# A selective scan taken by halves of the channels, with its decay in PSUM and another order on ScalarE

## The chip, the cores and the metric

The kernel runs on one core of one Trainium2 chip, as one program. The metric is the device time in microseconds (us). Its engines are TensorE (PE; PEld is its weight load), VectorE (DVE), ScalarE (ACT), GpSimd (POOL) and SyncE (SP).

## The reference

The program is eight stages: a Mamba-like selective scan, two kinds of mixture of experts, each twice, and three attention stages, over 1024 tokens of width 256. Each adds its result to the stream x. Only the first stage, the scan, is touched. With u the normed stream, delta a softplus of a small projection, and B and C two rows of 16 numbers for each token, it computes for each channel d and each of 16 states n

```python
def step(h, inp):
    u_t, delta_t, B_t, C_t = inp
    dA = jnp.exp(delta_t[:, :, None] * A)
    dBu = (delta_t * u_t)[:, :, None] * B_t[:, None, :]
    h = dA * h + dBu
    y_t = jnp.einsum('bdn,bn->bd', h, C_t)
    return (h, y_t)
```

and then y + u * D. The kernel here treats the 1024 tokens as two sequences of 512, in each of which the recurrence starts anew.

## The kernel before

The channels lie on the 128 partitions, as two halves (dc = 0, 1, NC = 2), and the tokens along the free axis, T = 1024 of them, as two sequences of SEQ = 512 (NSEQ = 2). The work of `selective_scan` has three parts.

**Ahead of the loop.** The stream is normed and transposed to g.xt, projected to `rows` (L313 copies them out of PSUM), and `rows` are projected to delta's argument in `wide` (L254). Softplus is made for each half of the channels in several steps: ScalarE takes Abs (L319), Exp (L324), Ln (L327) and Exp of the negative (L331), in each step for both halves before the next step; DVE takes the relu (L368), the correction for lost bits (L375 to L379), delta (L381) and delta times u, `du` (L382); POOL adds the two main parts (L230). Three table loads stand between ScalarE's steps (two of them ahead of L327 and L331, one ahead of the exponential of A, L321).

**The loop over the states.** It runs for n = 0 to 15, written as a hardware loop of 8 rounds with two states each (k = 0, 1). For a state:

- PE spreads row n of B and row n of C over all partitions, `spread` at L276, four bf16 matmuls of 512 columns into `wide[:, 0]` (B) and `wide[:, 1]` (C), B first. B waits until DVE has read the one before it (`driven`), C until ScalarE has copied the one before it (`copied`).
- ScalarE makes `decay` for both halves of the channels, exp(delta * A), 128x1024 each (L338), into SBUF, and then copies C's row out of PSUM into `cs` (L342), from which POOL reads it.
- DVE makes `drive` = du * B for both halves (L390, which reads B in PSUM), sets the decay at the first token of each sequence to zero (L393), and runs the recurrence over 1024 tokens for each half, `tensor_tensor_scan` at L398. All its operands but B lie in SBUF.
- POOL multiplies `state` with `cs` into `term`, for each half of the channels (L238), from SBUF to SBUF.
- PE adds `term` to `acc` in PSUM through the identity matrix in float32, `add_terms` at L284. An addition of one half of the channels is two matmuls in the program and four rows of the trace.

`decay`, `drive`, `state`, `term` and `cs` have two buffers each. PE's order is written out by hand: spread(n + 1), then add_terms(n). So PE spreads state n + 2 only once it has added state n.

**Behind the loop.** DVE adds u * D to `acc` (L406), PE transposes the result (L303), and DVE adds it to x (L411). The next stage begins with the norm at L106.

Of the kernel before, what the change touches and what calls it, by code (L numbers as in the profile page):

```python
# [5 lines left out]
F32 = mybir.dt.float32  # L6
BF16 = mybir.dt.bfloat16
# [5 lines left out]
P = 128  # L13
# [165 lines left out]
def selective_scan(nc, g, d):  # L179


    c = {n: Count(nc, n, p) for n, p in (
        ("loaded", 0), ("projected", 0), ("rows", 0), ("split", 0), ("dt", 0), ("soft_v", 0),
        ("size", 0), ("relu", 0), ("nega", 0), ("e", 0), ("lg", 0), ("over", 0), ("main", 0),
        ("ready", 0), ("spread_b", 0), ("spread_c", 0), ("copied", 0), ("decay", 0), ("driven", 0), ("state", 4),
        ("read", 4), ("summed", 4), ("gated", 0), ("turned", 0), ("zeroed", 0), ("selected", 0), ("added", 0))}
    HALF = 2 * N_STATE
    with (
        sbuf(nc, "xw", [P, NC, XROWS], F32) as xw,
        sbuf(nc, "dtw", [XROWS, H], F32) as dtw,  # L190
        sbuf(nc, "vecs", [P, 2 * NC + NC * N_STATE], F32) as vecs,
        sbuf(nc, "pick1", [3 * HALF, HALF], F32) as pick1,
        sbuf(nc, "pick", [3 * HALF, HALF, P], BF16) as pick,
        sbuf(nc, "rows", [XROWS, T], F32) as rows,
        sbuf(nc, "rest", [3 * HALF, T], F32) as rest,
        sbuf(nc, "part", [3 * HALF, T], BF16) as part,
        sbuf(nc, "stack", [3 * HALF, T], BF16) as stack,
        sbuf(nc, "nega", [P, NC, N_STATE], F32) as nega,
        sbuf(nc, "delta", [P, NC, T], F32) as delta,
        sbuf(nc, "du", [P, NC, T], F32) as du,  # L200
        sbuf(nc, "decay", [P, 2, NC, T], F32) as decay,
        sbuf(nc, "drive", [P, 2, NC, T], F32) as drive,
        sbuf(nc, "state", [P, 2, NC, T], F32) as state,
        sbuf(nc, "term", [P, 2, NC, T], F32) as term,
        sbuf(nc, "cs", [P, 2, T], F32) as cs,
        psum(nc, "acc", [P, NC, T], F32) as acc,
        psum(nc, "wide", [P, 2, T], F32) as wide,
        nc.Block() as block,
    ):
# [13 lines left out]
        def _(pool):  # L223
            pool.wait_ge(c["loaded"].sem, 64)
            pool.tensor_copy(pick[:, :, :], pick1[:, :].unsqueeze(2).broadcast_to([3 * HALF, HALF, P])) \
# [5 lines left out]
            pool.sem_inc(c["read"].sem, c["read"].prime)  # L231
            with pool.Fori(0, N_STATE // 2) as i:
                for k in range(2):
                    for dc in range(NC):
                        wait(pool, c["state"], 2 * k + dc + 1, i, 4)
                        wait(pool, c["copied"], k + 1, i, 2)
                        wait(pool, c["summed"], 2 * k + dc - 3, i, 4)
                        pool.tensor_tensor(term[:, k, dc, :], state[:, k, dc, :], cs[:, k, :], ALU.mult) \  # L238
                            .then_inc(c["read"].sem, 1)

        @block.tensor
        def _(pe):
# [3 lines left out]
            for s in range(NSEQ):  # L246
                for kc in range(NC):
                    last = pe.matmul(acc[0:XROWS, 0, s * SEQ:(s + 1) * SEQ], xw[:, kc, :],
                                     g.xt[:, kc, s * SEQ:(s + 1) * SEQ], start=(kc == 0), stop=(kc == NC - 1))
                last.then_inc(c["projected"].sem, 1)  # L250
# [1706 lines left out]
```

## Time and profile before

| | |
|---|---|
| median of 3 runs | 1935.83 us (1930.82 to 1942.93) |
| the profiled execution | 1939.39 us, span 1937.6 us |
| its mean granted clock of TensorE | 0.94 |
| PE, DVE, ACT, POOL busy over the span | 87%, 71%, 50%, 36% |
| the scan stage, up to the end of L411 | 198.5 us |

Times of rows are counted from the start of the span. A row gives a start, a duration, the engine, the line and the operation; x is how many instructions it groups; the brackets tell how long the engine had been idle and what released it. PEclk is the clock granted to TensorE, 1.00 for 2.4 GHz and 0.50 for 1.2 GHz.

### The profile page before, as it was taken

Reading aid. Unit: us, or ns where it says so; the run is one execution under the profiler, and the core shown is the slowest. Engines: PE = TensorE matmul, PEld = TensorE weight load, DVE = VectorE, ACT = ScalarE, POOL = GpSimd, SP = SyncE. Lnnn points to the kernel's source line nnn. Section 1 sums busy time; section 2 is a strip of 40 time slices with the busy share of each in tenths; the row PEclk is TensorE's granted clock in tenths of the full one; section 3 lists DMA queues with packets and bytes.
Section 4 is the critical chain, followed back from the end, with each engine's and each line's share of the span. In section 5 each row is a group of like instructions: output and inputs, shape, how many; then the busy total and the mean of one; then the engine's idle time right before and its main releaser. Section 6 shows DMA issues by size and latency. Waiting matters only on the chain. (4 is left out here: it accounts for less than half of the span.)

```text
span 1937.6 us, 35418 instructions
## 1 busy us (share of the span) xinstructions
PE 1688.6 (87%) x10848; PEld 1358.2 (70%) x10848; DVE 1380.8 (71%) x2841; ACT 976.3 (50%) x2160; POOL 691.8 (36%) x610
## 2 busy tenths in 40 slices
PE   2666799689999989989999998899799999888986
PEld 1222688567777978867777787777587888887764
DVE  6998666778887467677778747655788888657653
ACT  3432443377787344337778744111588888633111
POOL 1676122156665012216556512100355555303000
PEclk8788899899999989989999998999899999998998
DMA  0000111100000011110000004398211000011984
GB/s 29 0 0 0 47 49 49 47 20 16 22 16 1 1 55 43 46 50 25 22 14 24 4 1 119 106 258 257 74 28 30 30 27 16 1 66 54 260 243 145
DMA packets 39478, 111.15 MB, mean 57 GB/s; under 512 B 5504, under 2 KB 23664, under 8 KB 32240
## 3 DMA queue, kind: packets, MB, share of 16 engines
q1 hardware_dynamic: 39408, 110.26, 19.6%
q8 instruction: 39, 0.64, 0.1%
q14 instruction: 31, 0.25, 0.0%
HBM read 109.19 MB, written 1.05 MB: 57 GB/s over the span
## 5 line engine op out<-in xcount | busy, mean ns | idle before, releaser
L1294 POOL TENSOR_TENSOR xn<-xn 128x512 f32<-128x512 f32 x138 | 180.1, 1305 | 269.6 <-DVE xn L1189 269.6
L1280 POOL TENSOR_SCALAR prob<-prob,recip 128x256 f32<-128x256 f32 (+2 forms) x256 | 229.5, 913 | 69.7 <-DVE recip L1173 69.6
L1084 ACT ACTIVATE prob<-banks,peak 128x256 f32<-128x256 f32 (+3 forms) x384 | 190.5, 502 | 109.2 <-DVE peak L1164 103.6
L933 PE MATMUL banks<-pt,v 128*128 128x256 f32 (+3 forms) x768 | 204.3, 409 | 6.9 <-ACT pt L1019 6.9
L933 PEld LDWEIGHTS banks<-pt,v 128*128 128x128 f32 x768 | 145.2, 190 | 73.8 <-issue 31.8
L888 PE MATMUL banks<-k_hi,q_hi 128*128 128x256 f32 (+2 forms) x384 | 152.7, 398 | 27.9 <-DVE k_lo L1180 27.8
L1164 DVE TENSOR_REDUCE peak<-banks 128x1 f32<-128x256 f32 (+3 forms) x384 | 160.9, 446 | 18.1 <-PE banks L892 16.2
L568 POOL TENSOR_TENSOR gu_lo<-gu,gu_hi 128x512 fp32r<-128x512 f32 x36 | 46.7, 1298 | 295.2 <-ACT gu_hi L526 295.2
L909 PE MATMUL banks<-ident,prob 128*128 128x128 f32 x864 | 140.4, 279 | 3.2 <-DVE pt L1017 3.2
L1189 DVE TENSOR_TENSOR xn<-xn,ropes 128x512 f32<-128x512 f32 x138 | 124.3, 901 | 0.0
L1187 DVE TENSOR_TENSOR xn<-banks,ropes 128x512 f32<-128x512 f32 x138 | 95.2, 690 | 39.9 <-ACT xn L1052 39.6
L284 PE MATMUL acc<-term,ident 128*128 128x512 f32 x128 | 79.7, 771 | 50.2 <-POOL term L238 50.2
L537 ACT ACTIVATE silu<-gate 128x512 f32<-128x512 f32 x72 | 43.1, 599 | 159.3 <-PE up L489 159.1
L889 PE MATMUL banks<-k_lo,q_hi 128*128 128x256 f32 (+2 forms) x384 | 120.7, 314 | 0.0
L890 PE MATMUL banks<-k_hi,q_lo 128*128 128x256 f32 (+2 forms) x384 | 120.4, 314 | 0.0
L238 POOL TENSOR_TENSOR term<-state,cs 128x1024 f32<-128x1024 f32 x32 | 102.5, 3222 | 48.5 <-DVE state L398 48.5
L1231 DVE TENSOR_TENSOR xl<-o,xh 128x1024 fp32r<-128x1024 f32 x48 | 58.8, 1225 | 85.0 <-ACT xh L1131 85.0
L612 DVE SCALAR_TENSOR_TENSOR x<-outs,weight,x 128x256 f32<-128x256 f32 x288 | 115.7, 475 | 0.0
L596 DVE TENSOR_TENSOR inner<-silu,up 128x512 f32<-128x512 f32 x72 | 49.5, 687 | 92.9 <-ACT silu L537 92.9
L947 PE MATMUL banks<-wo_hi,xh 128*128 128x256 f32 x384 | 108.8, 283 | 0.4 <-DVE xl L1231 0.2
L1173 DVE RECIPROCAL recip<-sums 128x2 f32<-128x2 f32 (+1 forms) x256 | 40.9, 160 | 94.5 <-ACT prob L1084 91.1
L949 PE MATMUL banks<-wo_hi,xl 128*128 128x256 f32 x384 | 107.9, 281 | 0.0
(252 smaller groups left out, 5160.6 us busy)
## 6 DMA issues: line engine op xcount, KB each, us to landing
wgu<-in_w_gu SPq DMA_DIRECT2D x32, 1408.0 KB, 14.0
wd<-in_w_d SPq DMA_DIRECT2D x32, 704.0 KB
gu<-in_w SPq DMA_DIRECT2D x36, 256.0 KB, 2.7
wd<-in_w SPq DMA_DIRECT2D x36, 128.0 KB, 2.0
wkv<-in_mha_kv SPq DMA_DIRECT2D x16, 256.0 KB, 2.6
wq<-in_mqa_q SPq DMA_DIRECT2D x16, 128.0 KB, 2.0
wo<-in_mqa_o SPq DMA_DIRECT2D x16, 128.0 KB, 2.2
wq<-in_gqa_q SPq DMA_DIRECT2D x16, 128.0 KB, 2.1
```

What stands on the lines that cost most here:

```text
L612: last = dve.scalar_tensor_tensor(g.x[:, t, :], outs[:, t, :], weight[:, t, e], g.x[:, t, :], ALU.mult, ALU.add)
L888: pe.matmul(wide, q_hi, k_hi, start=True, stop=False)
L889: pe.matmul(wide, q_hi, k_lo, start=False, stop=False)
L890: pe.matmul(wide, q_lo, k_hi, start=False, stop=False)
L909: last = pe.transpose(t_bank[(NG * n + gi) % 2][:, at:at + P], prob[:, s, cols[t] + x * P:cols[t] + (x + 1) * P], g.ident[:, :])
L933: last = pe.matmul(o_bank[:, x * P:to], v[:, s, x, at:at + P], pt[:, s, x, first:first + to - x * P], start=(j == 0), stop=(j == NQ - 1))
L947: pe.matmul(to, o_hi, hi, start=(half == h == 0), stop=False)
L1084: last = act.activation(prob[:, s, cols[t]:cols[t] + n], s_bank[gi][:, psum_col[t]:psum_col[t] + n], ACT.Exp, bias=peak[:, s, t:t + 1], ac ...
L1164: last = dve.reduce_max(peak[:, s, t:t + 1], s_bank[gi][:, psum_col[t]:psum_col[t] + len(keys[t]) * P], axis=AX.X, negate=True)
L1189: dve.tensor_tensor(swap[:, r % 2, :], swap[:, r % 2, :], ropes[:, which, 1, :], ALU.mult) \
L1280: last = pool.tensor_scalar(part, part, recip[:, s, t:t + 1], None, ALU.mult)
L1294: pool.tensor_tensor(cosed[:, r % 2, :], cosed[:, r % 2, :], swap[:, r % 2, :], ALU.add) \
```

## The change

- The loop over the states runs once for each half of the channels: 32 units u = 16 dc + n in place of 16 states. A unit has one drive, one C copy, one term, one addition, all over 1024 tokens, and a spread of B and C of its own.
- `decay` lies in PSUM and has one buffer, of which each sequence's 512 tokens are made and used by themselves. ScalarE makes it with two activations of 512 columns, each after the scan of the same sequence of the unit before, and DVE scans each sequence by itself from 0.0. The memset at L393 is gone.
- On ScalarE the copy of C's row stands ahead of the unit's two decays.
- `acc` holds one half of the channels. It is cleared at the start of each half, for the second after DVE's `gate` has read it.
- DVE's gate of the first half stands behind the first scan of the second half. All transposes stand at the end, those of the first half ahead of the second's.
- Ahead of the loop: ScalarE takes the relu, makes all its steps for one half before the next, and loads one table set for Exp and Ln, before its first step. A's exponential is moved ahead of Abs. The temporary tiles no longer share memory with those of the loop.

The order of PE is still spread(u + 1), then add_terms(u).

```diff
+        drive = sb("drive", [P, 2, T], F32)
+        state = sb("state", [P, 2, T], F32)
+        term = sb("term", [P, 2, T], F32)
+        cs = sb("cs", [P, 2, T], F32)
+        mixed = sb("mixed", [P, NC, T], F32)
+        acc = ps("acc", [P, T], F32)
+        decay = ps("decay", [P, T], F32)
+        wide = ps("wide", [P, 2, T], F32)
...
-        size, e, lg, relu, over, lost = decay[:, 0], decay[:, 1], drive[:, 0], drive[:, 1], state[:, 0], state[:, 1]
+        LAST = N_STATE // 2 - 1
...
-            pool.sem_inc(c["read"].sem, c["read"].prime)
-            with pool.Fori(0, N_STATE // 2) as i:
-                for k in range(2):
-                    for dc in range(NC):
-                        wait(pool, c["state"], 2 * k + dc + 1, i, 4)
-                        wait(pool, c["copied"], k + 1, i, 2)
-                        wait(pool, c["summed"], 2 * k + dc - 3, i, 4)
-                        pool.tensor_tensor(term[:, k, dc, :], state[:, k, dc, :], cs[:, k, :], ALU.mult) \
-                            .then_inc(c["read"].sem, 1)
+
+            def read(i, u):
+
+                k = u % 2
+                wait(pool, c["state"], 2 * u + 2, i, 4)
+                wait(pool, c["copied"], u + 1, i, 2)
+                wait(pool, c["summed"], u - 1, i, 2)
+                pool.tensor_tensor(term[:, k, :], state[:, k, :], cs[:, k, :], ALU.mult).then_inc(c["read"].sem, 1)
+
+            read(0, 0)
...
+            def clear(dc):
+
                 for s in range(NSEQ):
-                    pe.matmul(acc[:, dc, s * SEQ:(s + 1) * SEQ], g.zeros[:, 0:P], g.zeros[:, :],
-                              start=True, stop=True)
-            pe.sem_inc(c["summed"].sem, c["summed"].prime)
-            pe.wait_ge(c["split"].sem, 1)
-            pe.wait_ge(c["selected"].sem, 1)
-
-            def spread(i, n):
+                    pe.matmul(acc[:, seq(s)], g.zeros[:, 0:P], g.zeros[:, :], start=True, stop=True)
...
+            def spread(i, u, n):
 
                 for which in range(2):
                     if which == 0:
-                        wait(pe, c["driven"], NC * n, i, 2 * NC)
+                        wait(pe, c["driven"], u, i, 2)
                     else:
-                        wait(pe, c["copied"], n, i, 2)
+                        wait(pe, c["copied"], u, i, 2)
...
-            def add_terms(i, k):
-                for dc in range(NC):
-                    wait(pe, c["read"], 2 * k + dc + 1, i, 4)
-                    for s in range(NSEQ):
...
-            LAST = N_STATE // 2 - 1
-            spread(0, 0)
-            with pe.Fori(0, LAST) as i:
-                for k in range(2):
-                    spread(i, k + 1)
-                    add_terms(i, k)
-            spread(LAST, 1)
-            add_terms(LAST, 0)
-            add_terms(LAST, 1)
-            for t in range(NT):
-                for dc in range(NC):
-                    if dc == 0:
-                        pe.wait_ge(c["gated"].sem, NSEQ * NC)
-                    last = pe.transpose(wide[:, t // 4, (t % 4) * H + dc * P:(t % 4) * H + (dc + 1) * P],
-                                        state[:, 0, dc, t * P:(t + 1) * P], g.ident[:, :])
...
+            def add_terms(i, u):
+                wait(pe, c["read"], u + 1, i, 2)
+                for s in range(NSEQ):
+                    last = pe.matmul(acc[:, seq(s)], g.ident[:, :], term[:, u % 2, seq(s)], start=False, stop=True,
+                                     skip_group_check=True)
+                last.then_inc(c["summed"].sem, 1)
...
+            pe.wait_ge(c["relu"].sem, NC)
+            spread(0, 0, 0)
+            for dc in range(NC):
+                base = dc * N_STATE
+                spread(0, base + 1, 1)
+                if dc:
+                    pe.wait_ge(c["gated"].sem, NSEQ * dc)
+                clear(dc)
+                add_terms(0, base)
+                with pe.Fori(0, LAST) as i:
+                    for k in range(2):
+                        spread(i, base + k + 2, k + 2)
+                        add_terms(i, base + k + 1)
+                if dc < NC - 1:
+                    spread(0, base + N_STATE, 0)
+                add_terms(LAST, base + 1)
+            pe.wait_ge(c["driven"].sem, NC * N_STATE)
+            pe.wait_ge(c["copied"].sem, NC * N_STATE)
+            for dc in range(NC):
+                for t in range(NT):
+                    pe.wait_ge(c["gated"].sem, NSEQ * dc + t // 4 + 1)
+                    pe.transpose(wide[:, t // 4, (t % 4) * H + dc * P:(t % 4) * H + (dc + 1) * P],
+                                 mixed[:, dc, t * P:(t + 1) * P], g.ident[:, :]).then_inc(c["turned"].sem, 1)
 
...
+            act.preload_act_table_set("natural_log_exp_and_others")
...
+            act.activation(nega[:, :, :], alog, ACT.Exp).then_inc(c["nega"].sem, 1)
...
+                act.activation(relu[:, dc, :], wide[:, dc, :], ACT.Relu, bias=bias[:, dc:dc + 1]) \
...
+                act.wait_ge(c["lg"].sem, dc + 1)
+                act.activation(size[:, dc, :], lg[:, dc, :], ACT.Exp, scale=-1.0).then_inc(c["over"].sem, 1)
+            act.wait_ge(c["minus"].sem, 1)
+
+            def decays(i, dc, n):
+
+                u = dc * N_STATE + n
+                at = slice(n, n + 1) if isinstance(i, int) else bass.ds(2 * i + n, 1)
+                wait(act, c["spread_c"], u + 1, i, 2)
+                wait(act, c["read"], u - 1, i, 2)
+                act.activation(cs[:, u % 2, :], wide[:, 1, :], ACT.Copy).then_inc(c["copied"].sem, 1)
+                for s in range(NSEQ):
+                    wait(act, c["state"], 2 * u - 1 + s, i, 4)
+                    act.sem_inc(c["paced"].sem, 1)
+                    act.activation(decay[:, seq(s)], delta[:, dc, seq(s)], ACT.Exp, scale=nega[:, dc, at]) \
+                        .then_inc(c["decay"].sem, 1)
+
             for dc in range(NC):
-
-                act.wait_ge(c["lg"].sem, dc + 1)
-                act.activation(over[:, dc, :], lg[:, dc, :], ACT.Exp, scale=-1.0).then_inc(c["over"].sem, 1)
-            act.wait_ge(c["ready"].sem, NC)
-            with act.Fori(0, N_STATE // 2) as i:
-                for k in range(2):
-                    for dc in range(NC):
-
-                        wait(act, c["state"], 2 * k + dc - 3, i, 4)
-                        act.activation(decay[:, k, dc, :], delta[:, dc, :], ACT.Exp,
-                                       scale=nega[:, dc, bass.ds(2 * i + k, 1)]).then_inc(c["decay"].sem, 1)
-                    wait(act, c["spread_c"], k + 1, i, 2)
-                    wait(act, c["read"], 2 * k - 2, i, 4)
-                    act.activation(cs[:, k, :], wide[:, 1, :], ACT.Copy).then_inc(c["copied"].sem, 1)
+                act.wait_ge(c["ready"].sem, dc + 1)
+                decays(0, dc, 0)
+                decays(0, dc, 1)
+                with act.Fori(0, LAST) as i:
+                    decays(i, dc, 2)
+                    decays(i, dc, 3)
 
...
-            for dc in range(NC):
-                dve.wait_ge(c["size"].sem, dc + 1)
-                dve.tensor_scalar(relu[:, dc, :], wide[:, dc, :], bias[:, dc:dc + 1], 0.0, ALU.add, ALU.max) \
-                    .then_inc(c["relu"].sem, 1)
...
             dve.wait_ge(c["ready"].sem, NC)
-            dve.sem_inc(c["state"].sem, c["state"].prime)
-            with dve.Fori(0, N_STATE // 2) as i:
-                for k in range(2):
-                    wait(dve, c["spread_b"], k + 1, i, 2)
-                    for dc in range(NC):
-                        wait(dve, c["state"], 2 * k + dc - 3, i, 4)
-                        dve.tensor_tensor(drive[:, k, dc, :], du[:, dc, :], wide[:, 0, :], ALU.mult) \
-                            .then_inc(c["driven"].sem, 1)
-                    wait(dve, c["decay"], 2 * (k + 1), i, 4)
-                    dve.memset(decay[:, k, :, 0:T:SEQ], 0.0).then_inc(c["zeroed"].sem, 1)
...
-                    for dc in range(NC):
-                        wait(dve, c["driven"], 2 * k + dc + 1, i, 4)
-                        wait(dve, c["read"], 2 * k + dc - 3, i, 4)
-                        dve.tensor_tensor_scan(state[:, k, dc, :], decay[:, k, dc, :], drive[:, k, dc, :], 0.0,
-                                               ALU.mult, ALU.add).then_inc(c["state"].sem, 1)
...
+            def scan(i, dc, n):
+
+                u, k = dc * N_STATE + n, n % 2
+                wait(dve, c["spread_b"], u + 1, i, 2)
+                wait(dve, c["state"], 2 * u - 2, i, 4)
+                dve.tensor_tensor(drive[:, k, :], du[:, dc, :], wide[:, 0, :], ALU.mult).then_inc(c["driven"].sem, 1)
+                wait(dve, c["driven"], u + 1, i, 2)
+                wait(dve, c["read"], u - 1, i, 2)
+                for s in range(NSEQ):
+                    wait(dve, c["decay"], 2 * u + s + 1, i, 4)
+                    dve.tensor_tensor_scan(state[:, k, seq(s)], decay[:, seq(s)], drive[:, k, seq(s)], 0.0,
+                                           ALU.mult, ALU.add).then_inc(c["state"].sem, 1)
+
+            def gate(dc):
+
+                wait(dve, c["summed"], (dc + 1) * N_STATE)
+                for s in range(NSEQ):
+                    dve.scalar_tensor_tensor(mixed[:, dc, seq(s)], g.xt[:, dc, seq(s)], dvec[:, dc:dc + 1],
+                                             acc[:, seq(s)], ALU.mult, ALU.add).then_inc(c["gated"].sem, 1)
 
             for dc in range(NC):
-                wait(dve, c["summed"], 2 * N_STATE - NC + dc + 1)
-                wait(dve, c["read"], 2 * N_STATE)
-                for s in range(NSEQ):
...
+                scan(0, dc, 0)
+                if dc:
+                    gate(dc - 1)
+                scan(0, dc, 1)
+                with dve.Fori(0, LAST) as i:
+                    scan(i, dc, 2)
+                    scan(i, dc, 3)
+            gate(NC - 1)
...
+                dve.wait_ge(c["turned"].sem, NT + t + 2)
```

## Rows read from the trace of the kernel before

**Rows 1.** Windows view, state loop: us, busy PE, PEld, DVE, ACT, POOL; PEclk, DMA share, GB/s

```profile
47.00:188.00 141.00, 88.28 (x180) 32.67 (x180) 137.25 (x80) 49.56 (x48) 99.82 (x31) 0.84 0.00 0
```

**Rows 2.** Lines view, 47 to 205 us: busy, mean ns of one, idle before

```profile
L238 POOL TENSOR_TENSOR term<-state,cs 128x1024 f32<-128x1024 f32 x32 | 102.5, 3222 | 48.5 <-DVE state L398 48.5
L398 DVE TENSOR_TENSOR_SCAN state<-decay,drive 128x1024 f32<-128x1024 f32 x32 | 100.8, 3188 | 0.7
L390 DVE TENSOR_TENSOR drive<-du,wide 128x1024 f32<-128x1024 f32 x32 | 37.2, 1201 | 1.4 <-PE wide L276 0.9 <-DVEq L384 0.4
L338 ACT ACTIVATE decay<-delta,nega 128x1024 f32<-128x1024 f32 x32 | 34.9, 1139 | 9.0 <-DVEq L384 9.0
...
L411 DVE TENSOR_TENSOR x<-x,wide 128x512 f32<-128x512 f32 x4 | 2.5, 680 | 0.8 <-PE wide L303 0.8
```

**Rows 3.** Timeline, 126 to 134.6 us, DVE against POOL: start, duration

```profile
126.77 2.34 POOL L238 TENSOR_TENSOR term<-state,cs 128x1024 f32<-128x1024 f32 x1
126.94 4.32 DVE L398 TENSOR_TENSOR_SCAN state<-decay,drive 128x1024 f32<-128x1024 f32 x1
...
131.18 2.26 DVE L398 TENSOR_TENSOR_SCAN state<-decay,drive 128x1024 f32<-128x1024 f32 x1
131.49 4.11 POOL L238 TENSOR_TENSOR term<-state,cs 128x1024 f32<-128x1024 f32 x1 [2.38 <-DVE state L398]
...
133.36 1.19 DVE L390 TENSOR_TENSOR drive<-du,wide 128x1024 f32<-128x1024 f32 x1
```

**Rows 4.** Timeline, 85 to 90 us: PE's burst and ScalarE behind it

```profile
85.16 1.98 PE L284 MATMUL acc<-term,ident 128*128 128x512 f32 x4 [0.33 <-POOL term L238]
...
86.98 1.03 PE L276 MATMUL wide<-stack,pick 96*128 96x512 bf16 x4
...
88.05 1.02 ACT L342 ACTIVATE cs<-wide 128x1024 f32<-128x1024 f32 x1 [3.65 <-PE wide L276]
88.97 2.18 ACT L338 ACTIVATE decay<-delta,nega 128x1024 f32<-128x1024 f32 x2
```

**Rows 5.** Timeline: PE at its lower clock, and after idle gaps

```profile
57.48 0.34 PEld L284 LDWEIGHTS acc<-term,ident 128*128 128x128 f32 x1 [0.52 <-issue]
58.33 0.34 PEld L284 LDWEIGHTS acc<-term,ident 128*128 128x128 f32 x1 [0.52 <-issue]
...
100.45 5.10 PE L284 MATMUL acc<-term,ident 128*128 128x512 f32 x8 [2.41 <-POOL term L238]
...
135.66 1.98 PE L284 MATMUL acc<-term,ident 128*128 128x512 f32 x4 [2.53 <-POOL term L238]
```

**Rows 6.** Timeline, 22 to 49 us: the steps ahead of the state loop

```profile
22.46 0.60 ACT L313 ACTIVATE rows<-acc 112x512 f32<-112x512 f32 x1 [1.12 <-PE acc L248]
...
25.20 1.11 ACT L319 ACTIVATE decay<-wide,vecs 128x1024 f32<-128x1024 f32 x1 [2.14 <-PE wide L254]
...
27.98 1.28 ACT L321 ACT_TABLE_LOAD   x1
29.27 0.23 ACT L321 ACTIVATE nega<-vecs 128x32 f32<-128x32 f32 x1
...
36.21 2.00 ACT L331 ACTIVATE state<-drive 128x1024 f32<-128x1024 f32 x2
37.37 3.38 DVE L379 TENSOR_TENSOR state<-state 128x1024 f32<-128x1024 f32 x1 [2.21 <-ACT state L331]
...
42.04 1.23 DVE L382 TENSOR_TENSOR du<-delta,xt 128x1024 f32<-128x1024 f32 x1
...
47.36 2.35 DVE L390 TENSOR_TENSOR drive<-du,wide 128x1024 f32<-128x1024 f32 x2 [0.44 <-DVEq L384]
```

**Rows 7.** Timeline, 179 to 199 us: the end of the scan stage

```profile
179.73 6.48 DVE L398 TENSOR_TENSOR_SCAN state<-decay,drive 128x1024 f32<-128x1024 f32 x2
...
193.84 1.41 DVE L406 SCALAR_TENSOR_TENSOR state<-xt,vecs,acc 128x512 f32<-128x512 f32 x2 [0.39 <-PE acc L284]
...
196.00 2.48 DVE L411 TENSOR_TENSOR x<-x,wide 128x512 f32<-128x512 f32 x4 [0.75 <-PE wide L303]
```

More of the change, by code:

```diff
@@ L179, in selective_scan @@
 def selective_scan(nc, g, d):
[L182 to L186, printed above, removed]
-    HALF = 2 * N_STATE
@@ L188, in selective_scan @@
[L188 to L209, printed above, removed]
+    c = {n: Count(nc, n) for n in (
+        "loaded", "projected", "rows", "split", "dt", "own", "size", "relu", "nega", "minus", "e", "lg", "over", "main",
+        "ready", "spread_b", "spread_c", "copied", "decay", "driven", "state", "read", "summed", "gated", "turned",
+        "selected", "paced")}
@@ new lines, in selective_scan, with sb, ps @@
+    HALF = 2 * N_STATE
+    A3 = 3 * HALF
+    with ExitStack() as ctx:
+        def sb(name, shape, dtype):
+            return ctx.enter_context(sbuf(nc, name, shape, dtype))
+        def ps(name, shape, dtype):
+            return ctx.enter_context(psum(nc, name, shape, dtype))
+        xw = sb("xw", [P, NC, XROWS], F32)
+        dtw = sb("dtw", [XROWS, H], F32)
+        vecs = sb("vecs", [P, 2 * NC + NC * N_STATE], F32)
+        pick1 = sb("pick1", [A3, HALF], F32)
+        pick = sb("pick", [A3, HALF, P], BF16)
+        rows = sb("rows", [XROWS, T], F32)
+        rest = sb("rest", [A3, T], F32)
+        part = sb("part", [A3, T], BF16)
+        stack = sb("stack", [A3, T], BF16)
+        nega = sb("nega", [P, NC, N_STATE], F32)
+        size = sb("size", [P, NC, T], F32)
+        e = sb("e", [P, NC, T], F32)
+        lg = sb("lg", [P, NC, T], F32)
+        relu = sb("relu", [P, NC, T], F32)
+        lost = sb("lost", [P, NC, T], F32)
+        delta = sb("delta", [P, NC, T], F32)
+        du = sb("du", [P, NC, T], F32)
+        drive = sb("drive", [P, 2, T], F32)
[6 more added lines that the diff above has]
+        wide = ps("wide", [P, 2, T], F32)
+        block = ctx.enter_context(nc.Block())
@@ L247, in _ @@
                 for kc in range(NC):
-                    last = pe.matmul(acc[0:XROWS, 0, s * SEQ:(s + 1) * SEQ], xw[:, kc, :],
-                                     g.xt[:, kc, s * SEQ:(s + 1) * SEQ], start=(kc == 0), stop=(kc == NC - 1))
+                    last = pe.matmul(acc[0:XROWS, seq(s)], xw[:, kc, :],
+                                     g.xt[:, kc, seq(s)], start=(kc == 0), stop=(kc == NC - 1))
                 last.then_inc(c["projected"].sem, 1)
@@ L275, in spread @@
                         lhs = pick[:, at, :].rearrange("p o m -> p (o m)")
-                        last = pe.matmul(wide[:, which, s * SEQ:(s + 1) * SEQ], lhs,
-                                         stack[:, s * SEQ:(s + 1) * SEQ], start=True, stop=True)
+                        last = pe.matmul(wide[:, which, seq(s)], lhs, stack[:, seq(s)], start=True, stop=True)
                     last.then_inc(c["spread_c" if which else "spread_b"].sem, 1)
-            def add_terms(i, k):
-                for dc in range(NC):
-                    wait(pe, c["read"], 2 * k + dc + 1, i, 4)
-                    for s in range(NSEQ):
-                        last = pe.matmul(acc[:, dc, s * SEQ:(s + 1) * SEQ], g.ident[:, :],
-                                         term[:, k, dc, s * SEQ:(s + 1) * SEQ], start=False, stop=True,
-                                         skip_group_check=True)
-                    last.then_inc(c["summed"].sem, 1)
@@ L376, in _ @@
                 link(dve.tensor_tensor(lost[:, dc, :], e[:, dc, :], lost[:, dc, :], ALU.subtract))
-            for dc in range(NC):
                 dve.wait_ge(c["over"].sem, dc + 1)
-                link(dve.tensor_tensor(lost[:, dc, :], lost[:, dc, :], over[:, dc, :], ALU.mult))
+                link(dve.tensor_tensor(lost[:, dc, :], lost[:, dc, :], size[:, dc, :], ALU.mult))
                 dve.wait_ge(c["main"].sem, dc + 1)
```

36 lines of the change are left out of this document (16 added, 20 removed).

## Prediction

> **What bounds the kernel now.** I read the windows view of the state loop first, then the groups by line, then the timeline. Only the scan stage is edited: 198.5 us of 1939.4. In the loop DVE is busy 137.25 of 141.00 us [rows 1], with next to no idle ahead of its scans and drives [rows 2], so DVE sets the pace: 8.80 us a state (six from the scan at 126.94 to that at 179.73 [rows 3, 7]). The work in that period is less than it seems. A scan's mean is 3188 ns [rows 2], but of two in a row one takes 4.32 and one 2.26 us [rows 3]. The long one starts 0.17 us after POOL's term and ends 2.15 after that term's end; then POOL's next term starts 0.31 after the second scan does, and takes 4.11, in place of 2.34. Each waits for the other. The drive, which has one operand in PSUM, takes 1.19 us beside a running term and makes nobody late [rows 3]. So with two SBUF inputs a scan and a term exclude each other, and a scan costs 2.26.
>
> **The loop by DVE's work.** `decay` in PSUM gives the scan one SBUF input, as the drive has; the drive's row is the nearest one, and by it the 2.1 us wait per state goes. A 512-column operation of two inputs takes 0.680 against 1.201 for 1024 [rows 2], which leaves 0.16 of fixed cost: a scan of 512 is (2.26 - 0.16) / 2 + 0.16 = 1.21 us (bounds 1.13, half of the whole, and 1.39, for as much again of fixed cost). A unit is then 1.20 + 1.21 + 1.17 = 3.6 us of DVE, 32 units 114, against 16 x 8.8 = 141. This would be the gain, if DVE stayed the bound.
>
> **The loop by its longest wait.** It doesn't, I think. PE spreads unit u + 2 only after it has added unit u. Follow that from the end E(u) of the unit's second scan:
>
> - to POOL's start 0.23 (126.94 + 4.32 = 131.26, and 131.49) and its term 2.34 [rows 3];
> - to PE 0.05 (131.49 + 4.11 = 135.60, and 135.66 [rows 5]); one addition to the start of the spread 1.82 (85.16 to 86.98), spread to C's copy 1.07 (88.05), copy to the first decay 0.92 (88.97) [rows 4];
> - a decay of 512: 1.14 [rows 2] less the 0.43 by which a copy of 512 (0.60 [rows 6]) is shorter than one of 1024 (1.02 [rows 4]), 0.71; to DVE 0.1 (the first of two at 36.21 ends some 1.05 later, DVE starts at 37.37 [rows 6]);
> - two scans, 1.21 + 1.17 (they overlap a little, as two drives of 1.20 take 2.35 [rows 6]). The second decay is ready before the second of them.
>
> Sum 9.62 us for two units, 4.81 a unit, against 3.6 by DVE's work. ScalarE's copy stands in this chain because it is put ahead of the decays; before, the decays were made ahead of it. The drive hangs on B, which is spread first: even by the end of the whole spread it is done at 0.23 + 2.34 + 0.05 + 1.82 + 1.07 + 1.20 = 6.7, ahead of the scan at 7.2, and so costs nothing; without the copy ahead it would come next, and the chain be 9.1 at most. Before, the same chain had 17.6 us for two states and only just fitted.
>
> This is at the higher clock. At 1.2 GHz weight loads of the addition stand 0.85 apart (57.48, 58.33 [rows 5]), so its four rows take 3.4 in place of 1.7, and the spread's four take 0.86 more: 12.2 us for the chain, 6.1 a unit. The granted clock was 0.84 over the loop [rows 1], low for a third of it. PE ran a burst at 1.2 GHz after an idle gap of 2.41 us (8 matmul rows in 5.10) and one at 2.4 GHz after 2.53 (4 in 1.98) [rows 5]; the new loop's gap is 4.8 - 2.7 = 2.1 us at the higher clock, close to these. I take the same 0.84: the 2.6 us of clocked work become 2.6 / 0.84 = 3.1, the chain 10.1, a unit 5.06. Ends: 9.62 and 12.2.
>
> The Trainium skill (TensorE: Matmul & The Clock Gate, on HAM oscillation) says that short bursts between recurring idle gaps make the clock fall again and again. The trace agrees (0.84 in [rows 1]). That is a rule against this change, since PE, which was off the path, now stands on it.
>
> **Ahead of the loop.** ScalarE's rows end at 23.06, PE's projection releases it at 25.20 [rows 6]. The one table load (1.28) and A's exponential (0.23) fit between, and cost nothing. Then, for the first half: Abs, relu, Exp, Ln, Exp, each some 1.05, the last two waiting 0.1 for the one before: last end 30.8. The second half: 36.2. Table loads taken off the path, three of 1.28, 3.85 us. DVE: the first half's correction waits for POOL's main sum, about 30 to 32.3 (before, its product took 3.38 beside that same sum [rows 6]), and ends at 33.6, delta 34.8, du 36.1. The second half's correction by 38.0, then its product, delta and du at 1.23 each [rows 6]: 41.8. First drive at 41.95, before at 47.36: -5.4 us (bounds -3, if POOL's second sum meets DVE's again, and -7).
>
> The Trainium skill (ScalarE: Activation LUTs, on what a table load costs) gives 2.66 us for a switch of sets, with a drain. The rows show 27.98 to 29.27, load and next start, with no drain [rows 6]. By the page the three loads would be 8.0 us.
>
> **From first drive to the end of the stage.** Unit 0: E(0) = 41.95 + 3.6 = 45.6. Unit 1 waits for PE at the lower clock (it has been idle), 2.0 us from drive's end at 43.2 to the copy, then 0.92 + 0.81 + 2.38: E(1) = 49.3. The first chains meet the low clock, as the loop did before; between 10.1 and 12.2 I take 11.1: E(3) = 60.4. Fourteen more chains: 14 x 10.1 = 141.4. The change of halves: gate (1.41) waits for the addition, 4.6 us behind E(15), and so drive 17 ends 0.4 late; the 0.4 us for clearing is hidden, since POOL's term of unit 16 ends later. E(31) = 202.2. Behind it: 0.23 + 2.34 + 0.05 + 2.0 to the gate, 1.41 + 0.1 + 2.48 [rows 7] to the end, with half of the transposes made beside the gate: 8.6 us. Before, it was 198.5 - 186.2 = 12.3, with two terms, two additions and two gates [rows 7]. End at 210.8, before 198.5: **+12 us**. (First drive to last scan: 160.3 against 138.9, +21.4; ahead -5.4; behind -3.7.) Nothing after the stage changes. The profiled execution, 1939.4, becomes 1952; it lies 3.6 above the median of 1935.8, which becomes **1948**, +0.6%.
>
> **The rivals.**
>
> - *DVE stays the bound.* If PE's spread were not late, 31 x 3.6 + 45.6 + 8.6 = 165.8, the stage 33 us shorter: 1903. It decides from a chain of 7.2 us down. For it: PE is busy only 2.7 of 4.8 us. Against: the sum above has 2.4 us too much, and no row of it is doubtful by that. Chance 0.10.
> - *The clock stays up.* 14 chains of 9.62, and the rest as above: 60.4 + 134.7 + 0.4 + 8.6 = 204.1, +6 us, 1941. For it: the gaps shrink from up to 3.6 to 2.1. Against: the row with the gap of 2.41. Chance 0.12.
> - *PE is low for over half of the time, or the chain has further waits* (0.1 at each of seven hand-overs). With half, 2.6 / 0.75 makes the chain 10.5, +18 us; with seven times 0.1 more, +28; always low, +43: 1955 to 1979. For it: a mean that is only carried over, and a copy, two decays and two scans with waits of their own. Against: in a low stretch the chain leaves PE hardly idle, and after such stretches the rows return to 2.4 GHz. Chance 0.28.
> - *The scan still collides with the term,* PSUM or not. In the chain the term runs from 0.23 to 2.57 behind E(u), and unit u + 1's scans from about 2.4: they hardly meet, at most 0.2 a unit, +6. It lies within the forecast.
>
> **The numbers.** My forecast, the chain at a mixed clock, has 0.50 and spans +6 to +18: 1942 to 1954 by itself. A difference of 1%, 19 us, is about what a measurement of this kernel can tell from none. Faster by more: the first rival, 0.10. Slower by more: the third, but for its mildest part, and a tail of the forecast: 0.30. The rest, 0.60, is within 1%. The range 1928 to 1976 takes in the second rival and nearly all of the third, and leaves out the first and the worst of the clock.
>
> **What the profile of the changed kernel would show.** If right: DVE idle about 1.3 us a unit ahead of its scans, waiting for ScalarE's decay; ScalarE's copy waiting for PE's spread, PE for POOL's term, without another wait longer than these; each term about 2.34 and each scan 1.2 long with no 4 us ones; first drive near 42, the stage's end near 211. Wrong if units come every 3.6 us with DVE over 90% busy, if scans of 512 take 2 us or more, if table loads still stand in the softplus, or if granted clock in the loop is far from 0.84.

## The result, and the profile after

The changed kernel takes 1986.2 us (median of 4 runs, 1967.4 to 1991.0), the one before 1939.4 (4 runs, 1930.8 to 1952.3): 1.022 of the time, with a 95% interval of 1.013 to 1.031. It is slower, and lies above the upper end of the forecast range (1976); whether the loss is over 2% stays open. The profiled execution took 1991.0 us, its span 1989.2. The scan stage holds most of it: the next stage's first instruction on DVE (L106) starts at 237.8 us, before at 199.6, which makes +38.2; the forecast was +12.

The windows view after, of the first 48 us and of the loop (columns as in [rows 1]). The line that answers to [rows 1] is the second:

```profile
0.00:48.00 48.00, 15.82 (x38) 7.38 (x39) 33.53 (x52) 18.42 (x22) 9.79 (x7) 0.84 0.09 29
48.00:220.00 172.00, 113.51 (x239) 43.23 (x238) 104.84 (x92) 64.91 (x87) 70.36 (x30) 0.78 0.00 0
```

And the groups of the loop that answer to [rows 2] (lines view, 45 to 250 us):

```profile
L251 POOL TENSOR_TENSOR term<-state,cs 128x1024 f32<-128x1024 f32 x32 | 75.1, 2345 | 116.4 <-DVE state L416 112.2 <-ACT cs L357 4.2
L416 DVE TENSOR_TENSOR_SCAN state<-decay,drive 128x512 f32<-128x512 f32 x64 | 74.8, 1210 | 18.6 <-ACT decay L361 16.1 <-DVE drive L411 2.5
...
L411 DVE TENSOR_TENSOR drive<-du,wide 128x1024 f32<-128x1024 f32 x32 | 38.7, 1209 | 50.1 <-PE wide L291 50.0
L357 ACT ACTIVATE cs<-wide 128x1024 f32<-128x1024 f32 x31 | 31.7, 1023 | 113.4 <-PE wide L291 113.4
```

What the edit is made of works: a term takes 2.35 us always, a scan of 512 takes 1.21, and nobody waits for the other. DVE's work in the loop fell from some 139 us to 114. But DVE now idles 50 us ahead of its drives, for PE's spread, and 19 ahead of its scans. It went from 97% busy to 61%. The waits follow each other around a ring: DVE for PE (L291), PE for POOL's term, POOL for DVE's state, ScalarE for PE.

One turn of it (timeline, 128 to 141 us; start, duration):

```profile
128.15 2.34 DVE L416 TENSOR_TENSOR_SCAN state<-decay,drive 128x512 f32<-128x512 f32 x2 [0.83 <-ACT decay L361]
...
130.74 2.35 POOL L251 TENSOR_TENSOR term<-state,cs 128x1024 f32<-128x1024 f32 x1 [5.03 <-DVE state L416]
131.81 2.34 DVE L416 TENSOR_TENSOR_SCAN state<-decay,drive 128x512 f32<-128x512 f32 x2 [0.21 <-DVE drive L411]
133.14 3.78 PE L297 MATMUL acc<-term,ident 128*128 128x512 f32 x4 [4.17 <-POOL term L251]
...
136.71 1.91 PE L291 MATMUL wide<-stack,pick 96*128 96x512 bf16 x4
...
138.42 2.01 PE L297 MATMUL acc<-term,ident 128*128 128x512 f32 x4
138.72 1.02 ACT L357 ACTIVATE cs<-wide 128x1024 f32<-128x1024 f32 x1 [7.42 <-PE wide L291]
...
139.64 1.29 ACT L361 ACTIVATE decay<-delta,nega 128x512 f32<-128x512 f32 x2
...
140.46 2.34 DVE L416 TENSOR_TENSOR_SCAN state<-decay,drive 128x512 f32<-128x512 f32 x2 [1.43 <-ACT decay L361]
```

From scan to scan of the even unit it is 12.31 us: scans 2.34, hand-overs and term 2.65, then PE's addition up to the spread 3.57, spread to copy 2.01, copy to decay 0.92, decay to scan 0.82. The forecast's chain has the same links, and all but PE's agree within 0.1 us. The odd unit starts 3.66 us behind the even one, at DVE's own pace, and its addition stands right behind the even unit's spread. So PE is busy in one burst for both and idle for 4.17 us. Most bursts begin at 1.2 GHz; the others fall to it in their first microsecond. This turn is the longest of the 14: the others take 11.0 to 12.2 us, mostly 11.3 and 12.2 in turn.

### The profile page after: what moved, and what is told of

Same layout as the page of the kernel before. It is cut to its first block and busy times, and to the rows that moved or that the text cites. A ratio compares the mean times of both kernels' runs of the same rounds, so it can differ in the third digit from the quotient of the medians.

```text
span 1989.2 us, 35845 instructions
## 1 busy us (share of the span) xinstructions
PE 1729.3 (87%) x10912; PEld 1379.4 (69%) x10912; DVE 1358.2 (68%) x2855; ACT 999.1 (50%) x2208; POOL 665.3 (33%) x610
## 5 line engine op out<-in xcount | busy, mean ns | idle before, releaser
L297 PE MATMUL acc<-term,ident 128*128 128x512 f32 x128 | 89.4, 837 | 59.7 <-POOL term L251 59.7
L251 POOL TENSOR_TENSOR term<-state,cs 128x1024 f32<-128x1024 f32 x32 | 75.1, 2345 | 116.4 <-DVE state L416 112.2
L975 PE MATMUL banks<-wo_lo,xh 128*128 128x256 f32 x384 | 107.8, 281 | 0.0
```

## The experiments

All that follow are the changed kernel with one edit, unless said otherwise. "Pair" is the time from an even unit's scan to that of the next even unit, as a mean over the 14 pairs between unit 2 and unit 30; "steady" leaves out the first pair and those at the change of halves (with them, pe_ahead has 7.53, ahead_behind 7.48 and warm 9.73); "L106" is where the next stage begins.

| kernel | pair, us | granted clock, 50 to 160 us | L106, us | median, us | ratio to before, 95% |
|---|---|---|---|---|---|
| before (a state in place of a pair) | 8.80 | 0.82 | 199.6 | 1939.4 | |
| changed | 11.66 | 0.78 (48 to 220) | 237.8 | 1986.2 | 1.022 [1.013, 1.031] |
| pe_ahead | 7.32 (steady) | 0.98 | 173.5 | 1920.9 | 0.987 [0.978, 0.995] |
| copy_behind | 10.30 | 0.81 | 216.1 | 1973.5 | 1.013 [1.004, 1.021] |
| warm | 9.60 (steady) | 0.95 | 211.1 | 1959.5 | 1.007 [1.002, 1.012] |
| ahead_sbuf | 9.58 (steady) | 0.91 | 208.6 | 1958.9 | 1.006 [1.000, 1.011] |
| spaced | 11.28 | 0.81 | 233.4 | 1994.4 | 1.024 [1.016, 1.031] |
| ahead_behind | 7.32 (steady) | 0.97 | 172.7 | 1918.0 | 0.986 [0.981, 0.992] |
| drive_ahead | 8.7 to 10.3 | 0.85 | 210.5 | 1954.7 | 1.007 [1.003, 1.011] |
| sbuf_only | 11.71 | 0.78 | 240.3 | 1992.6 (one run) | |
| warm_behind | 9.03 | 0.97 | 200.7 | 1968.6 (one run) | |
| warm_less | 10.99 | 0.83 | 229.4 | 1984.3 (one run) | |
| before_ahead | 8.80 | 0.82 | 199.5 | 1935.9 (one run) | |

Each ratio is against runs of the kernel before on the same chip, whose medians lay between 1939 and 1948 us. L106 comes from one trace of each kernel. It is free of the scatter of the other stages, told of below, which whole times carry: warm_behind's stage is 10 us shorter than warm's, and its one run 9 us longer than warm's median. But the start of the first scan differs between 45.0 and 47.7 us among kernels with the same code up to there, so a difference in L106 of 2 us is nothing by itself.

**PE's order (pe_ahead).**

```diff
+            spread(0, 1, 1)
             for dc in range(NC):
                 base = dc * N_STATE
-                spread(0, base + 1, 1)
...
-                add_terms(0, base)
                 with pe.Fori(0, LAST) as i:
                     for k in range(2):
                         spread(i, base + k + 2, k + 2)
-                        add_terms(i, base + k + 1)
+                        add_terms(i, base + k)
...
```

> The changed kernel, with PE's order turned: spread(u + 2), then add_terms(u), where it was add_terms(u), then spread(u + 2). Nothing else is changed. Chain theory (PE's spread stands behind the addition and so behind GpSimd's term): the spread of u + 2 is then free at the end of drive u + 1, and units come at DVE's work, 1.2 + 2.34 and hand-overs = 3.7 us in place of the 5.8 seen; 32 units in 118 us, the scan stage near 172 us in place of 237, the kernel 64 us faster than the changed one and some 15 to 27 faster than the one before. Rival (the doubled spreads and copies, or PSUM as the scan's source, are dear in themselves): the unit stays above 5 us and the stage above 210.

A unit came every 3.66 us once the loop was steady, L106 fell from 237.8 to 173.5, and the kernel takes 0.987 of the time of the one before. Around its steady state (timeline, 99 to 103 us):

```profile
100.63 1.04 PE L291 MATMUL wide<-stack,pick 96*128 96x512 bf16 x4 [0.20 <-DVE drive L411]
100.78 2.34 DVE L416 TENSOR_TENSOR_SCAN state<-decay,drive 128x512 f32<-128x512 f32 x2 [0.21 <-ACT decay L361]
...
102.12 1.98 PE L297 MATMUL acc<-term,ident 128*128 128x512 f32 x4 [0.45 <-POOL term L251]
```

The spread now goes as soon as the drive ahead of it is done, and PE's idle is in pieces of 0.2 and 0.45 us, so that it keeps 2.4 GHz (0.98). The position of two lines of PE's program was worth 62 us of the loop (64 of L106, of which 2.2 lie ahead of the first scan). Some 27 of them could be had by the clock alone, as warm will show. The doubled spreads and copies, the rival, cost nothing that is seen.

**The same in the kernel before (before_ahead).** There the edit is spread(n + 2) ahead of add_terms(n).

> The kernel before with PE's order turned in the same way as in pe_ahead (spread of n + 2, then the addition of n). Chain theory: before, PE was not on the path, DVE was: the state keeps 8.8 us and the stage 198.5, within 2 us. Rival (PE's order was already costing time before): the stage gets shorter by more than 5 us, and the gain of pe_ahead would not be owed to the new loop.

The state kept 8.80 us and L106 is 199.5. PE's order was harmless as long as DVE needed 8.8 us for a state, and it is the new loop that makes it the bound.

**ScalarE's copy (copy_behind).** `decays` makes the two decays first and then the copy.

```diff
             def decays(i, dc, n):
...
+                for s in range(NSEQ):
+                    ...
                 wait(act, c["spread_c"], u + 1, i, 2)
                 wait(act, c["read"], u - 1, i, 2)
                 act.activation(cs[:, u % 2, :], wide[:, 1, :], ACT.Copy).then_inc(c["copied"].sem, 1)
-                for s in range(NSEQ):
-                    ...
```

> The changed kernel, with ScalarE's copy of C's row put behind the unit's two decays. Chain theory: the copy's 0.92 us leave the chain, the drive comes next; DVE's idle before scans that ScalarE's decay ended, 16.1 us in all, goes: 11 to 16 us off the scan stage (237 to about 223). Rival (the copy's place is indifferent, since C's row is needed by GpSimd as early as the decay by DVE): 0 to 3 us.

The pair fell by 1.36 us and L106 by 21.7, of which 2.1 lie ahead of the first scan: more than the 0.8 that the chain gives. The shorter chain also leaves a shorter gap on PE. In three pairs in a row it was 3.55, 2.74 and 2.48, and the bursts behind it began at 1.2, 2.4 and 1.2 GHz (granted clock 0.50, 1.00, 0.50); the pair with the fast burst was 2.2 us shorter than the one ahead of it (8.98 and 11.19). Timeline, 100 to 130 us, PE:

```profile
103.47 3.78 PE L297 MATMUL acc<-term,ident 128*128 128x512 f32 x4 [3.55 <-POOL term L251]
...
114.67 1.98 PE L297 MATMUL acc<-term,ident 128*128 128x512 f32 x4 [2.74 <-POOL term L251]
...
123.64 3.47 PE L297 MATMUL acc<-term,ident 128*128 128x512 f32 x4 [2.48 <-POOL term L251]
```

So part of this gain is the clock's, which the next runs set apart.

**The clock (warm).** In the hardware loops, behind the spread of each odd unit, where PE is idle:

```diff
                         spread(i, base + k + 2, k + 2)
+                        for f in range(12 if k else 0):
+                            pe.matmul(acc[:, seq(f % 2)], g.zeros[:, 0:P], g.zeros[:, :], start=False, stop=True,
+                                      skip_group_check=True)
```

> The changed kernel, with 12 further matmuls that add zeros to acc (128x512 bf16, 0.21 us each at 2.4 GHz) behind the spread of every odd unit in the hardware loops, where PE is idle for 4.17 us. The result is the same. Clock theory: the granted clock in the loop goes from 0.78 to above 0.95, each pair's first addition takes 1.8 in place of 3.2 to 3.4 and its spread 0.9 in place of up to 1.7; the pair goes from 11.66 to about 9.6 us, 14 pairs save 25 to 30 us: the stage near 208. Rival (clock is a side effect, the pair's length comes from the order of the waits): 0, or slower by up to 10 where the filler delays an addition.

Once the clock was up, every pair took 9.60 us, but for the one across the change of halves (11.30), where loop and filler end; the forecast's sum at 2.4 GHz was 9.62. Timeline, 106 to 113 us:

```profile
107.20 2.34 DVE L419 TENSOR_TENSOR_SCAN state<-decay,drive 128x512 f32<-128x512 f32 x2 [0.84 <-ACT decay L364]
...
109.79 2.36 POOL L251 TENSOR_TENSOR term<-state,cs 128x1024 f32<-128x1024 f32 x1 [3.61 <-DVE state L419]
...
112.20 1.98 PE L297 MATMUL acc<-term,ident 128*128 128x512 f32 x4 [0.52 <-POOL term L251]
...
114.02 1.03 PE L291 MATMUL wide<-stack,pick 96*128 96x512 bf16 x4
```

Addition to spread is 1.82 us again, in place of 2.9 to 3.6. Work that computes nothing saved 27 us: this is the clock's price here, 2.06 us a pair, with the order of all waits unchanged.

**Both (warm_behind).**

> The changed kernel with the 12 zero matmuls of warm and ScalarE's copy behind the decays. At a steady 2.4 GHz the chain's sum can be read without the clock: with the copy ahead a pair took 9.60 us in warm. With it behind, the drive comes next, which starts 0.74 behind the spread's start and takes 1.2: the pair is 0.8 us shorter, 8.8, the stage 11 to 13 us shorter than warm's 210. Rival (the 1.36 us a pair that copy_behind gained came from the clock, not from the chain): the pair stays at 9.6 here.

A pair takes 9.03 as a mean, 8.97 between 94.6 and 103.6: 0.6 less than warm, not 0.8, as the scan waits 0.21 for the drive right before it; L106 is 10.4 below warm's. So of copy_behind's 1.36 us a pair some 0.6 is the copy's place and the rest the clock.

**Less filler (warm_less).** 5 zero matmuls in place of 12.

> As warm, with 5 zero matmuls in place of 12: PE's gap of 4.17 us is cut by 1.1 us at 2.4 GHz, by 2.1 at 1.2. If the clock falls by the gap's length alone, as I took from the rows of the kernel before (kept after 2.53, fallen after 2.41 and after 3.65), a gap of 2.1 to 3.1 leaves it mixed: granted 0.80 to 0.90, pairs of 10 to 11 us, stage 215 to 228. Rival: even this little holds the clock, pairs 9.6 and the stage near 210; or it does nothing, 11.6 and 237.

Mixed, as expected, and at the upper edge of what was expected: some pairs of 9.6, some of 11.1 to 12.3, clock 0.83. But the rule in the expectation, that the gap's length alone decides, is refuted. After one gap of 2.03 us the addition ran at 2.4 GHz, after the next of that length at 1.2; after gaps of 3.08 the clock was up at 74.85 us and down at 105.32 (timeline, 84 to 110 us, PE):

```profile
84.45 1.98 PE L297 MATMUL acc<-term,ident 128*128 128x512 f32 x4 [2.03 <-POOL term L251]
...
94.05 3.66 PE L297 MATMUL acc<-term,ident 128*128 128x512 f32 x4 [2.03 <-POOL term L251]
...
105.32 3.78 PE L297 MATMUL acc<-term,ident 128*128 128x512 f32 x4 [3.08 <-POOL term L251]
```

**Even spacing (spaced).** The forecast assumed a gap of 2.1 us, which needs units at even distances.

```diff
                 u, k = dc * N_STATE + n, n % 2
+                for t in range(3 if k else 0):
+                    dve.bn_stats(g.bn[:, t, :], g.x[:, t, :])
                 wait(dve, c["spread_b"], u + 1, i, 2)
```

> The changed kernel, with three bn_stats of 0.36 to 0.41 us on DVE ahead of each odd unit's drive, whose results nothing in this stage uses. They part the two units of a pair: 1.1 + 1.2 + 2.34 = 4.8 us from even to odd unit in place of 3.66. The prediction assumed just this spacing, and a granted clock of 0.84. Spacing theory (the clock falls because both additions of a pair stand together and leave PE idle for 4.17 us): with the gap halved to about 2 us the clock goes above 0.78, the pair from 11.66 to between 9.7 and 10.4, the stage from 237 to 210 to 219, though DVE has 18 us more to do. Rival (more work on DVE costs time, and the clock falls at gaps of 2 us as well): the pair stays above 11 us.

This expectation failed. The odd unit's scans did come 4.64 us behind the even ones, but PE's gap only went from 4.17 to 3.85, and the pair stayed at 11.28, as a mean:

```profile
103.79 2.34 DVE L418 TENSOR_TENSOR_SCAN state<-decay,drive 128x512 f32<-128x512 f32 x2 [1.25 <-ACT decay L361]
...
106.05 1.05 DVE L410 BATCH_NORM_STATS2 bn<-x 128x6 f32<-128x256 f32 x3
...
108.43 2.34 DVE L418 TENSOR_TENSOR_SCAN state<-decay,drive 128x512 f32<-128x512 f32 x2 [0.21 <-DVE drive L413]
108.78 3.24 PE L297 MATMUL acc<-term,ident 128*128 128x512 f32 x4 [3.85 <-POOL term L251]
```

At 1.2 GHz the even unit's addition and spread last until the odd unit's term is there, whether that unit comes 3.66 or 4.64 us later. The two additions join into one burst, and the gap behind them is the rest of the even unit's chain. As I read it, the slow clock makes the gap by which it comes back.

The same trace also shows what the forecast assumed, units at nearly even distances with the clock up. After the change of halves the granted clock was 1.00 from 147 to 174 us, PE's gaps were 1.2 to 2.1 us, with one of 2.68, and two pairs took 9.60 us. Then, behind a gap of 2.13, it fell, and the pairs were 11.1 to 12.2 again (timeline, 153 to 186 us, PE):

```profile
164.32 1.98 PE L297 MATMUL acc<-term,ident 128*128 128x512 f32 x4 [2.12 <-POOL term L251]
...
173.93 3.52 PE L297 MATMUL acc<-term,ident 128*128 128x512 f32 x4 [2.13 <-POOL term L251]
```

So even spacing didn't hold the clock in this run, and the low clock can come back without a gap of 4 us.

**Where decay lies (sbuf_only, ahead_sbuf).** `decay = sb("decay", ...)` in place of `ps`, in the changed kernel and in pe_ahead.

> The changed kernel, with decay in SBUF in place of PSUM and nothing else: one part of the change undone. Port theory within the chain: scans of the odd unit wait for the even unit's term (second unit of a pair 1.3 us later), terms stay at 2.35; the even unit's chain, which sets the pair's length, hardly feels it: pair 11.7 to 12.7 us, stage 0 to 16 us longer than 237. So decay in PSUM would buy little here. Rival (PSUM is what costs): the stage gets shorter.

> As pe_ahead, and decay lies in SBUF in place of PSUM, in the same size and with the same waits. Port theory (a scan with two SBUF inputs and GpSimd's term exclude each other): the scan of unit u + 1 would begin 1.25 us behind the end of unit u, and the term of u lasts till 2.6 behind it: first scans of 512 take about 2.5 in place of 1.21, the unit goes from 3.7 to about 5, the stage is 40 us longer than with pe_ahead. Rival (where decay lies matters little once the pace is free of PE): the same time as pe_ahead within 5 us.

In the changed kernel decay in PSUM is worth 2.5 us of L106, about what two traces differ by. The odd unit starts 3.66 us behind the even one, as before, and not 1.3 later as expected; its scans are longer, but they are off the chain (timeline of sbuf_only):

```profile
110.33 3.47 DVE L416 TENSOR_TENSOR_SCAN state<-decay,drive 128x512 f32<-128x512 f32 x2 [0.21 <-DVE drive L411]
```

With PE's order turned decay in PSUM is worth 35.1 us of L106 (208.6 against 173.5), of which 1.9 lie ahead of the first scan. Timeline of ahead_sbuf, 101 to 107 us, where the scans wait for the term that started 1.09 us ahead of them:

```profile
101.97 2.35 POOL L251 TENSOR_TENSOR term<-state,cs 128x1024 f32<-128x1024 f32 x1 [2.43 <-DVE state L416]
...
103.06 3.46 DVE L416 TENSOR_TENSOR_SCAN state<-decay,drive 128x512 f32<-128x512 f32 x2 [0.21 <-DVE drive L411]
```

Two scans take 3.46 in place of 2.34. The Trainium skill (SBUF — State Buffer, Who interferes with whom) says that a DVE instruction with two SBUF inputs contends with a GpSimd instruction that reads SBUF, and that one with at most one SBUF input, outside DVE's 2-port modes, doesn't; the two traces agree (3.46 and 2.34).

**Both orders (ahead_behind).**

> Both turned: PE's spread(u + 2) ahead of add_terms(u), and ScalarE's copy behind the two decays. Chain theory: with PE's order turned DVE sets the pace at 3.66 us a unit, and the copy's place is worth nothing: within 3 us of pe_ahead (stage 172). Rival (GpSimd, which already waits 24.7 us in all for ScalarE's copy in pe_ahead, gets C's row too late when the copy stands behind): 10 us or more slower than pe_ahead.

L106 at 172.7 against 173.5, and 1918.0 us: the same as pe_ahead within what is measured. This is the fastest version, 0.986 of the kernel before.

**One step further (drive_ahead).** On top of pe_ahead, DVE makes the drive of u + 1 ahead of the scans of u.

```diff
-                    scan(i, dc, 2)
-                    scan(i, dc, 3)
+                    for k in range(2):
+                        drive_of(i, dc, k + 3)
+                        scan(i, dc, k + 2)
...
```

> As pe_ahead, and DVE makes the drive of unit u + 1 ahead of the scans of unit u, so that no scan waits for the drive right before it. Theory (DVE alone sets the pace in pe_ahead): its idle of 0.21 us ahead of each first scan goes, a unit takes 3.45 in place of 3.66, the stage is 6 us shorter than with pe_ahead, near 166. Rival (ScalarE's copy and decays, or the wait of ScalarE for GpSimd's term, come next at once): no gain, or a loss.

This expectation failed: it lost 37 us of L106, 2.2 of them ahead of the first drive. I had looked at ScalarE and at GpSimd for the next wait, and it was PE again (timeline, 104 to 110 us):

```profile
104.71 3.55 PE L297 MATMUL acc<-term,ident 128*128 128x512 f32 x4 [3.24 <-POOL term L251]
...
108.83 1.22 DVE L411 TENSOR_TENSOR drive<-du,wide 128x1024 f32<-128x1024 f32 x1 [3.20 <-PE wide L291]
...
109.97 2.33 DVE L420 TENSOR_TENSOR_SCAN state<-decay,drive 128x512 f32<-128x512 f32 x2
```

Drive u + 3 now stands ahead of scan u + 2, and needs the spread of u + 3, which stands behind the addition of u. By asking one unit earlier, DVE gave back the distance that pe_ahead had won.

## Why the prediction was wrong

*The mechanism* was right: PE's spread behind its addition closes a ring through POOL, ScalarE and DVE, which takes the place of DVE's work. pe_ahead takes the way from addition to spread out of it, copy_behind the copy, and warm the low clock; the links of POOL and DVE are read from the waits. The sign in the sum (+12) was right too, though the forecast called it "within 1%" and it came out at 2.2% (1.3 to 3.1).

*The step that failed* is "I take the same 0.84: ... the chain 10.1". The chain at 2.4 GHz was right to 0.02 us (warm). The clocked part was mis-sized. The mean clock in the loop was 0.78, not far from 0.84, but a mean over time was the wrong quantity: the clock is low at the start of most bursts, or falls within the first microsecond. That start is the even unit's addition and spread, which are on the chain; for the odd unit's, which aren't, the clock is mostly high. The chain's PE links, 2.89 us at 2.4 GHz, took 4.4 to 5.6, while a mean of 0.84 would make them 3.4 and one of 0.78 would make them 3.7. Measured pair 11.66, forecast 10.1; 14 pairs make 21.8 us. Behind it lies the gap: "4.8 - 2.7 = 2.1" assumed evenly spaced units, and it was 3.7 to 4.2. The gap alone doesn't explain the clock, though: warm_less and spaced lost it after gaps of 2.03 and 2.13 us too. The trace of before should have warned: in each of the five bursts after a gap of 3.65 us the clock is low from the start or falls in its first 1.4 us, and a chain of two units that start 3.66 apart by DVE's pace, as my own E(0) = 45.6 and E(1) = 49.3 say, leaves PE one long gap.

*By part,* with what I forecast in brackets. The first drive and the last scans (timeline of the changed kernel):

```profile
46.06 1.22 DVE L411 TENSOR_TENSOR drive<-du,wide 128x1024 f32<-128x1024 f32 x1
...
225.85 2.34 DVE L416 TENSOR_TENSOR_SCAN state<-decay,drive 128x512 f32<-128x512 f32 x2 [0.21 <-DVE drive L411]
```

From the one to the end of the other 182.1 us (160.3). The tail, from there to L106, 9.6 against 13.4 before, -3.8 (-3.7). Ahead of the loop, from ScalarE's first step at 27.02 to the first drive at 46.06, 19.0 against 22.2 before, -3.1 (-5.4, with -3 as a bound). That bound's reason came true in another place: POOL's second sum met not DVE's work for the second half but the first half's du, which took 3.25 in place of 1.23. The first half's product took 3.26 beside POOL's first sum, which the forecast had nearly allowed for (timeline, 31 to 41 us):

```profile
31.42 3.34 POOL L243 TENSOR_TENSOR relu<-relu,lg 128x1024 f32<-128x1024 f32 x1 [17.72 <-ACT lg L346]
...
32.58 3.26 DVE L400 TENSOR_TENSOR lost<-lost,size 128x1024 f32<-128x1024 f32 x1
...
36.63 2.67 POOL L243 TENSOR_TENSOR relu<-relu,lg 128x1024 f32<-128x1024 f32 x1 [1.87 <-ACT lg L346]
37.14 3.25 DVE L403 TENSOR_TENSOR du<-delta,xt 128x1024 f32<-128x1024 f32 x1
```

The remaining 1.8 us are a late start: ScalarE's first step began at 27.02, before at 25.20, since the eight rows of PE's first projection took 5.58 us in this execution and 3.66 in that of before, as if at the lower clock; in others of the changed kernel's kin the first scan comes 2 us earlier. Together 43.3 - 3.8 - 3.1 + 1.8 = 38.2. Of the 26 us by which the stage missed its forecast, 21.8 are the loop's, 2.3 the part ahead of it, and 1.8 the late start. The single table load was hidden, as forecast, and the others are gone. The switch of halves cost 1.1 us (second scan 4.80 behind the first, in place of 3.66) on the odd unit, and nothing on the chain.

*Outside the stage* the profiled executions differ by another 13.4 us (1989.2 - 237.8 against 1937.6 - 199.6), where nothing was edited and I had forecast nothing. The sixth stage, a mixture of experts, took 189.7 us before and 195.3 after, and between 188.2 and 213.1 in the thirteen traces; in the longest but one PE's weight loads waited 20.4 us for the experts' weights (6.0 before). The seventh, an attention stage, took 362.7 and 366.9, in all 361.1 to 367.1, at a granted clock of 0.94 to 0.97. The last stage took 204.2 and 207.1, in all 189.6 to 210.9. None of them follows the pair's length. In the seventh stage the two traces of the old loop are the shortest, by 1.6 us or more; why is open. The measured +47 us of the medians are thus about 38 of the stage and 9 of this, as far as one trace of each kernel tells.

*The rivals.* The third, low clock and further waits, was the nearest by price: +38 lies between its "half of the time" (+18) and "always low" (+43). But neither of its conditions was met. A mean of 0.78 is a low clock for 44% of the time, and the hand-overs were within 0.1 us of the forecast; what counted was where in the burst the low clock fell. The second (the clock stays up) is what warm made, 11.5 us of L106 above before. The first (DVE stays the bound) would have needed the order of pe_ahead. The fourth didn't happen: terms took 2.35 us and scans 1.21 throughout.

## What to carry to other kernels

When an edit shortens the bounding engine's work, write down the ring of waits that runs through every in-order queue, and divide it by the number of units that are in flight. Here two units in flight and a ring of 9.6 us made 4.8 a unit out of DVE's 3.66, and issuing the producer (the spread) ahead of the consumer (the addition) on the third engine turned a loss of 2.2% into a gain of 1.3%. If TensorE stands on the ring, price it at the clock of those bursts that are on the ring, here the ones behind its longest gap, and not at the mean.

## What the runs showed of the hardware

- In the loops of the thirteen traces TensorE's clock was low at the start of the burst, or fell in its first 1.4 us, after every gap of 3.2 to 4.5 us. After 0.52 us it was up (warm). Between them the length of the gap alone doesn't tell: up after 2.53 [rows 5] and 2.74, down after 2.41 [rows 5] and 2.48, and both up and down after 2.03 and after 3.08 (warm_less). Filling a gap of 4.17 us with products of zeros kept it up and took 27 us off the stage. The Trainium skill (TensorE: Matmul & The Clock Gate, on HAM oscillation) describes such a loop, in which short bursts between recurring gaps let the clock fall again and again; the changed kernel's 0.78 agrees. New to me was that the slow burst lengthens the ring and joins two bursts into one. That it so keeps up the gap that slows it is my reading: no run sets it apart from a clock that falls at the shorter gaps of a fast ring as well, as it did in spaced and warm_less.
- A scan of 512 columns takes 1.21 us with its first operand in PSUM, and two take 2.34; the fixed cost of 0.16 from an addition and a drive held for the scan. With both operands in SBUF two take 2.34 as well where no term runs beside them (sbuf_only, even units), and 3.46 where one does.
- ScalarE writes 512 exponentials to PSUM in 0.69 us and to SBUF in 0.71 (sbuf_only) to 0.72 (ahead_sbuf).
